# Query-key similarity as one rounded pass over 96 stacked rows, with four orders changed around it

## What is computed

```
normed = layernorm(x) * ln_w + ln_b
v, gate = split(silu(normed @ W_hidden.T + b_hidden))
Z = silu(normed @ W_qk.T + b_qk)            # 32 wide
q = Z * gamma[0] + beta[0];  k = Z * gamma[1] + beta[1]
A = square(relu(q @ k.T / 256))
t = t + ((A @ v) * gate) @ W_out.T + b_out + x
router_logits = t' @ Wr.T                   # 8 experts, the two largest are taken
out = softmax(top2) weighted sum of gelu(t' @ Wi.T + bi) @ Wo.T + bo
```

## Time and profile before

| | |
|---|---|
| median of 3 runs | 595.96 us |
| profiled execution, its own time | 593.35 us |
| span of that execution, first to last instruction | 591.3 us |
| mean granted clock of TensorE | 0.993 |
| PE busy | 561.2 us (95%) |
| VectorE (DVE) busy | 378.1 us (64%) |
| ScalarE (ACT) busy | 330.1 us (56%) |
| GpSimd (POOL) busy | 275.1 us (47%) |

### The profile page before, as it was taken

One profiled execution on the slowest core, in us unless ns is written; L12 is line 12 of the kernel. 1 busy time (PEld: TensorE's weight loads), 2 busy tenths in 40 slices (PEclk: granted clock), 3 DMA queues, 4 the chain that ended last, 5 costly groups with the idle time before them and its releaser, 6 DMA issues. The chain is left out here.

```text
span 591.3 us, 13846 instructions
## 1 busy us (share of the span) xinstructions
PE 561.2 (95%) x3812; PEld 533.3 (90%) x3813; DVE 378.1 (64%) x1428; ACT 330.1 (56%) x723; POOL 275.1 (47%) x314
## 2 busy tenths in 40 slices
PE   1899999989999999999899999999999999999993
PEld 0889998778888888888899999999999999999993
DVE  4568677587776777787887455555555555556660
ACT  2343333846667666665774556655555566555640
POOL 2433322016646656566474455545444555544542
PEclk9999999999999999999999999999999999999997
DMA  8980000401112111112244333323333333223211
GB/s 286 406 328 2 2 1 21 161 14 61 62 40 72 49 55 65 41 64 86 69 115 62 55 47 48 48 47 53 53 54 54 45 49 51 43 34 46 38 28 20
DMA packets 31835, 42.49 MB, mean 72 GB/s; under 512 B 4596, under 2 KB 27797, under 8 KB 31670
## 3 DMA queue, kind: packets, MB, share of 16 engines
q0 software_dynamic: 13488, 13.74, 14.7%
q1 hardware_dynamic: 18196, 28.16, 14.2%
q10 hardware_dynamic: 114, 0.15, 0.1%
HBM read 24.46 MB, written 17.57 MB: 71 GB/s over the span
## 5 line engine op out<-in xcount | busy, mean ns | idle before, releaser
L871 ACT ACTIVATE hT<-ps,b_i_sb 128x256 f32<-128x256 f32 (+1 forms) x240 | 94.3, 448 | 113.9 <-PE ps L1427 113.7
L1427 PE MATMUL ps<-w_o_sb,hT 128*128 x852 | 146.8, 329 | 0.9 <-ACT hT L871 0.9
L1427 PEld LDWEIGHTS ps<-w_o_sb,hT 128*128 128x128 f32 x852 | 139.2, 192 | 1.3 <-issue 1.3
L737 POOL DMA_INDIRECT out_rows<-const,y_row x71 | 126.5, 1782 | 27.5 <-issue 27.5
L1427 PE MATMUL ps<-n_hi,we_hi 128*128 128x256 f32 (+1 forms) x468 | 124.6, 289 | 1.1 <-DVE we_lo L1308 1.1
L1427 PE MATMUL ps<-n_hi,we_lo 128*128 128x256 f32 (+1 forms) x468 | 92.8, 280 | 0.0
L1427 PEld LDWEIGHTS ps<-n_hi,we_hi 128*128 128x128 f32 x468 | 88.7, 190 | 1.4 <-DVE we_lo L1308 1.4
L1308 DVE TENSOR_TENSOR we_lo<-we_all,we_hi 128x768 fp32r<-128x768 f32 x80 | 73.1, 955 | 14.4 <-issue 13.5
L1427 PEld LDWEIGHTS ps<-n_hi,we_lo 128*128 128x128 f32 x468 | 71.5, 189 | 0.0
L852 ACT ACTIVATE we_hi<-we_all 128x768 fp32r x80 | 63.5, 849 | 3.9 <-DVE tile_expert L1246 2.4
L1427 PE MATMUL ps<-nA_lo,we_hi 128*128 128x256 f32 (+1 forms) x234 | 65.5, 280 | 0.0
(11 more groups left out here) (242 smaller groups left out, 1088.9 us busy)
## 6 DMA issues: line engine op xcount, KB each, us to landing
we_all<-in_w_i SPq DMA_DIRECT2D x8, 768.0 KB, 12.6
conv_only<-lists SPq DMA_DIRECT2D x31, 194.0 KB, 2.8
w_o_sb<-in_w_o SPq DMA_DIRECT2D x8, 576.0 KB, 18.1
out_rows<-X SPq DMA_DIRECT2D x16, 192.0 KB
X<-in_x SPq DMA_DIRECT2D x1, 1536.0 KB, 10.3
out_rows<-const,y_row POOLq DMA_INDIRECT x71, 3.7
conv_only<-lists SPq DMA_DIRECT2D x9, 97.0 KB, 2.0
we_all<-in_w_hid SPq DMA_DIRECT2D x1, 776.0 KB, 6.5
```

The lines of the kernel that those rows point to most:

```text
L737: pool.indirect_dma_start(out=out, out_offset=bass.IndirectOffsetOnAxis(ap=y_row[:, odd, t:t + 1], axis=0), in_=y_sb[:, odd, t, :], in_off ...
L871: last = act.activation(hT[:, odd, f, 0:n].unsqueeze(1), ps_h[:, b, c, 0:n].unsqueeze(1), ACT.Gelu, bias=b_i_sb[:, ds(e * FCHUNKS + f, 1)])
L1427: return pe.matmul(dst, lhsT, rhs, start=start, stop=stop)
```

## The change

Query and key are made in parts, stacked on 96 partitions, and the similarity is one float32r product over 96 rows. The z weights and gamma and beta are stored three times, so z comes out as three copies on 96 rows. ACT writes rounded values of q (three copies) into `q_parts`, of k into `k_parts`, and the unrounded q, k, q into `qk_full`; DVE then subtracts, on one band of 32 rows each, the rounded from the unrounded value, so that the 96 rows hold q and k in the combinations high by high, high by low, low by high:

The rest of the diff, cut to its core (buffers of 32 rows become 96; `weighted_b_o` moves into `attnT`):

```
-                        last = mm(ps_sim[:, t, :], kT[:, t * P:(t + 1) * P], qT[:, :])
+                        last = mm(ps_sim[:, t, :], k_parts[:, t * P:(t + 1) * P], q_parts[:, :])
-                products(ps_z, w_qk_hi, w_qk_lo, slice(0, QK), False).then_inc(z_ps, 1)
+                products(ps_z, w_qk_hi, w_qk_lo, slice(0, QK3), False).then_inc(z_ps, 1)
 
+            def logits_of_base(i, odd):            # now ScalarE, two homes: from_base[:, odd]
+                wait(act, out_read, i - 1)
+                for t in range(HALVES):
+                    last = act.activation(from_base[:, odd, t, :], ps_vr[:, t, HID:VR], ACT.Copy,
+                                          scale=a_scale[:, ds(i * HALVES + t, 1)])
+                last.then_inc(l1_done, 1)
...
                     act.activation(v_sb[:, :, :], ps_v, ACT.Silu).then_inc(v_done, 1)
+                    logits_of_base(i, odd)
...
+                if not absent(i + 2) and not (isinstance(i, int) and i < 0):
+                    normalise(i + 2)
                 if not absent(i + 1):
                     act.wait_ge(z_ps, i + 2)
                     act.activation(zT[:, :], ps_z, ACT.Silu).then_inc(z_done, 1)
-                if not absent(i + 2):
+                    query_key_high(i + 1)
+                if isinstance(i, int) and i < 0:
                     normalise(i + 2)
```

More of the change, by code:

```diff
@@ L270, in build @@
         nB_bias = sb("nB_bias", [KBB, SEQ], f32r)
-        zT, qT, kT = (xc[0:QK, :, :, :].rearrange("p a t c -> p (a t c)")[:, n * SEQ:(n + 1) * SEQ] for n in range(3))
+        zT, qk_full = (xc[0:QK3, :, :, :].rearrange("p a t c -> p (a t c)")[:, n * SEQ:(n + 1) * SEQ] for n in range(2))
+        Q_LOW, K_LOW = slice(2 * QK, QK3), slice(QK, 2 * QK)
+        q_parts = sb("q_parts", [QK3, SEQ], f32r)
+        k_parts = sb("k_parts", [QK3, SEQ], f32r)
         hT = sb("hT", [P, 2, FCHUNKS, TWO])
@@ L686, in _, with put_rows @@
                 conv_step(p)
+            def put_rows(c, rows):
+                for t in range(HALVES):
+                    pool.indirect_dma_start(
+                        out=lists, out_offset=bass.IndirectOffsetOnAxis(ap=slots[:, c, t:t + 1], axis=0),
+                        in_=rows[:, t, :], in_offset=None).then_inc(scattered, 16)
             def attn_step(i):
                 r = i - 1
[L690 to L694, removed]
                 if not absent(i):
@@ L714, in attn_step @@
                     pool.wait_ge(slots_done, r + 1)
[L715 to L719, removed]
+                    put_rows(0, row_a)
+                if not absent(i):
+                    wait_alone(pool, u_var_done, i + 1, ld_const)
+                    wait(pool, u_done, i)
+                    pool.tensor_tensor(u_pow[:, :], u_var[:, :], minus_half[:, :], ALU.pow).then_inc(u_pow_done, 1)
+                if not absent(r):
+                    put_rows(1, row_b)
             pool.wait_ge(ld_attn, 16 * 5)
@@ L1248, in store_table, with finish_tokens @@
                 dve.wait_ge(tiles_done, 2 * n + 2)
-            def finish_tokens(r):
+            def finish_tokens(r, odd):
                 dve.wait_ge(out_ps, r + 1)
@@ L1332, in attn_step @@
                     twin(2, 0)
-                if not absent(i):
-                    logits_of_base(i)
                 if not absent(r):
                     logits_of_tokens(r)
-                    choose(r)
                 if not absent(i + 1) and not under_conv(i + 1):
@@ L1350, in attn_step @@
                                           ALU.mult).then_inc(gated_done, 1)
+                if not absent(r):
+                    choose(r)
                 if last_image(r):
@@ L1376, in _ @@
             dve.wait_ge(ld_rest, 16)
-            pipeline(dve, attn_step, **ATTN, chain=chain, per=8)
+            pipeline(dve, attn_step, **ATTN, parity=True, chain=chain, per=9)
             dve.tensor_copy(list_end[:, :], list_at[:, :]).then_inc(ends_done, 1)
@@ L1669, in attn_step @@
                     pe.wait_ge(tiles_done, 2)
-                if not absent(r):
-                    pe.wait_ge(in_row_done, r + 1)
-                    wait(pe, prefix_read, r)
-                    mm(ps_rows_before, before_bf[:, :], in_row[:, :])
-                    mm(ps_rows_all, ones_bf[:, :], in_row[:, :]).then_inc(prefix_ps, 1)
                 if not absent(i + 1):
@@ L1685, in attn_step @@
                     last.then_inc(out_ps, 1)
+                if not absent(r):
+                    pe.wait_ge(in_row_done, r + 1)
+                    wait(pe, prefix_read, r)
+                    mm(ps_rows_before, before_bf[:, :], in_row[:, :])
+                    mm(ps_rows_all, ones_bf[:, :], in_row[:, :]).then_inc(prefix_ps, 1)
             pipeline(pe, attn_step, **ATTN)
@@ L1740 @@
     w_i = np.ascontiguousarray(two_parts(L1_ffn_Wi).transpose(2, 0, 1, 3).reshape(P, EXPERTS, 2 * FF))
-    w_qk = np.ascontiguousarray(two_parts(L1_attn_W_qk).swapaxes(0, 1))
+    w_qk = np.ascontiguousarray(np.tile(two_parts(L1_attn_W_qk).swapaxes(0, 1), (1, 1, 3)))
     b_i = np.asarray(L1_ffn_bi).reshape(EXPERTS * FCHUNKS, P)
```

73 lines of the change are left out of this document (39 added, 34 removed).

## The result

The changed kernel took a median of 602.60 us in 7 runs (598.90 to 604.11), the kernel before 595.96 in 7 (594.65 to 598.04). The ratio is 1.010, interval 1.007 to 1.013. The forecast was 589.5, its range 585 to 597: wrong in sign, and outside the range. The profiled execution took 602.6 us, its span 600.2.

The account below looks back on a forecast made before the run. PE, busy 95% of the span, was taken as the bound. 13 periods of 0.83 give 10.8, less 2.3 at the start and 2.0 at the end: 6.5 us, so 586.85 profiled, plus 2.61: 589.5 us, range 585 to 597.

Parts of the forecast that it names:

- DVE ... it fits: Attention stage, VectorE: with `choose` behind the gated product, 2.7 us free per image now, 1.9 at a period of 9.9.
- PE, the gain: Attention stage, similarity: two records instead of four, 0.79 us saved; period 9.9, or 0.83 less per image.
- ACT, the price: Attention stage, ScalarE: three passes 1.58 us and the base's columns 0.40 per image, 9.4 of 9.9 busy.
- ACT is dearer: Rival, ScalarE in the attention stage: base's columns cost 0.62, ScalarE sets a period of 10.15, about 592.5 us; chance 0.18.
- The ring of scatters: GpSimd, from `row_a` through four scatters to the next: 8.97 us, 9.73 with `u_pow`, 0.17 below the period.
- The start: First images of the attention stage: passes push image 0's similarity by 1.6, image 1 loses 0.7, together 2.3 us lost.
- The end: Last images to the first expert tile: `choose` before the low weights 1.1, less slack for tables 0.9, together 2.0 us lost.
- the slower one: Rival, GpSimd's scatters set 10.65, about 599 us; or similarity not at one-pass pace, about 600; together chance 0.10.
- Better: Rival, attention stage: gaps around the similarity go too, period 9.7, start partly won back, gain 10, 585.9 us; chance 0.12.

Follow-up runs that it names:

- the run without the hold: The changed kernel with the output bias added to X by VectorE, in front of query and key, instead of by GpSimd: 591.85 us, ratio 0.9922.
- the third experiment: The changed kernel with one order undone, `u_pow` behind all four scatters again: 599.88 us.

## Why the prediction was wrong

**The step that failed** is "DVE ... it fits". It weighed VectorE's free time, 2.7 per image, against its work, and took 1.9 to be left. The work itself came to 7.8 per image in the run without the addition, within the 8.0 counted with (0.5 of which was hold already); but the new orders and the shorter period put more of VectorE's instructions with operands in SBUF beside GpSimd's addition, and 1.5 per image went there (1.71 - 0.19, 1.68 - 0.15), on the path from the scatters back to the scatters. No single order does it: with `choose` or `u_pow` put back alone, VectorE is still held. Run by run: without the addition, 593.64 and neither of the two held; with the same addition on VectorE, 591.85; in the kernel before, no effect. The trace of before had the sign (0.67 where the next step has 0.16), and I read past it, because a held instruction is counted as busy.

**PE, the gain:** the records came at the pace of z, as taken (0.24 against 0.27 for two). A period in which PE has no hole is 10.03, so 0.70 is saved and not the 0.83 that I took; 13 x 0.13 = 1.7 us too much.

**ACT, the price:** the three passes run from 199.78 to 201.36, 1.58 as taken (the terms of the sum, 3 x 0.587 less 2 x 0.1, make 1.56). Two of the base's columns take 0.42 until done, 0.30 in the queue; I had 0.49 and 0.40. "ACT is dearer" is refuted: ScalarE is busy 9.1 of 10.03 in the run without the addition, where PE is busy 20.04 of 20.05. The columns and the passes in the changed kernel, ahead of them the tanh step that the part on the rivals needs:

```profile
191.91 0.20 ACT L953 ACTIVATE tanh_d<-diff 128x2 f32<-128x2 f32 x1 [1.53 <-DVE diff L1327]
...
193.99 0.42 ACT L875 ACTIVATE from_base<-ps,a_scale 128x8 f32<-128x8 f32 x2
...
199.78 0.60 ACT L867 ACTIVATE q_parts<-xc,gb_sb 96x256 fp32r<-96x256 f32 x1
200.29 0.58 ACT L867 ACTIVATE k_parts<-xc,gb_sb 96x256 fp32r<-96x256 f32 x1
200.78 0.58 ACT L867 ACTIVATE xc<-xc,gb_sb 96x256 f32<-96x256 f32 x1
```

**The ring of scatters** is shorter than the period, as taken: the gap behind `u_pow` is 0.18 and not 0.30 or 0.97. It binds at 10.7 when the addition is put in front of the last scatters.

**The start:** 2.3 was taken. Free of the hold it is 1.45 in front of image 0's similarity (1.6 taken) and 2.82 up to image 2's (0.7 taken): 4.3. What I had not put behind the subtractions is VectorE's 6.2 us for the scales of images 12 to 15: they delay the low parts for which PE then waits 3.9. With the scales moved, this stretch is 4.8 shorter.

**The end:** free of the hold, images 12 to 15 win 0.94 instead of 3 x 0.70 = 2.1, and the last stretch loses 0.95: 2.1 lost, 2.0 taken.

With these sizes the sum is 13 x 0.70 = 9.1, less 4.3, less 2.1: a gain of 2.7, and the run without the hold shows 2.44 in the table. The frame of the sum held; a term was missing from it, the hold, 8.9 us by the table and 10.7 by the medians.

**The rivals:** the slower one had the right engine, GpSimd, and nearly the right time (599 to 600), but not the mechanism: ScalarE does wait 1.53 in front of tanh (191.91 above), yet for VectorE's `diff`, not for the scatters. So it was wrong as well. "Better" came nearest to what the study ended with (585.9 against 587.46), by other means.

## What to carry to other kernels

Before you move a VectorE instruction, note which of its neighbours read two operands in SBUF and when GpSimd computes: a held instruction shows as a long one, and not as a wait, so compare its duration with that of its twin in another image. Free time of an engine is a sum over the image; what counts is whether the instruction is through when the next engine asks, as the 14.4 us of the base's columns show. An order should be judged once the main disturbance is gone: in the changed kernel, undoing an order seemed to win 2 to 3 us, and without the hold each of three orders turned out to be worth 3 to 8.

## What was not expected of the hardware

The hold begins before the addition does in the profile: the compare started at 189.07, the addition's record at 189.71, when GpSimd was still in a scatter's record (from 188.73). With `u_pow` in front of the addition it is the same: in the third experiment `in_first` is held from 191.06, the addition's record starts at 191.48. A scatter by itself doesn't hold such instructions: without the addition, `chosen` at 196.96 and the newton step at 197.38 took 0.19 and 0.16 while a scatter's record ran from 196.50 to 197.46. Whether the addition takes hold when it is queued, or its record starts late, wasn't tried; the profile's page calls GpSimd's spans rough.

Scatters aren't without effect on VectorE, though. `u_neg`, which reads one tile (195.77, above), took 0.33 instead of 0.17 and ended at 196.10, 0.03 before the record of a scatter from 195.13 did. This is seen in many images, small, and its cause is open.

The first products of the convolution run at half pace for 2 us longer in some executions than in others, in changed and unchanged kernels alike, with 1.00 in the column of the granted clock in that stretch. It is a part of what runs of one kernel differ by, and wasn't looked into.
